# Issuing the next tile's q, k, v projection ahead of the feed-forward's down products in a two-layer transformer kernel

## The reference, cut to what matters

```python
def _layer(x, wqkv, qs, ksc, wo, lg, lb, w1, b1, w2, b2):
    h = shift_token(x)
    q, k, v = split(h @ wqkv, 3)            # 8 heads of 64
    q = l2norm(q) * qs ; k = l2norm(k) * ksc
    q, k = rotary_xpos(q, k)
    o = local_attention(q, k, v)            # windows of 64, each sees itself and the one before
    x = x + o @ wo
    h = layernorm(shift_token(x)) * lg + lb
    a, g = split(h @ w1 + b1, 2)            # hidden width 341
    return x + (a * gelu(g)) @ w2 + b2
```

## Time and profile before

| what | value |
|---|---|
| median of 3 runs | 470.61 us (469.17 to 472.55) |
| the profiled execution | 471.67 us |
| its span, first to last instruction | 469.9 us |
| granted TensorE clock, mean share | 0.916 |
| PE busy | 359.3 us (76%) |
| DVE busy | 329.7 us (70%) |
| POOL busy | 298.2 us (63%) |
| ACT busy | 285.0 us (61%) |

### The profile page before, as it was taken

How to read it: one execution, slowest core, us unless ns; L and a number is a source line. 1 busy time by engine, 2 the same in 40 slices (tenths; PEclk the granted TensorE clock), 3 DMA queues, 4 the chain that set the end, 5 groups by cost and what they waited for, 6 DMA issues and landing times.

```text
span 469.9 us, 11254 instructions
## 1 busy us (share of the span) xinstructions
PE 359.3 (76%) x3832; PEld 295.0 (63%) x3832; DVE 329.7 (70%) x744; ACT 285.0 (61%) x852; POOL 298.2 (63%) x248
## 2 busy tenths in 40 slices
PE   2573057898788998899899989998949896768362
PEld 1352036777676877687778767876838775656342
DVE  6879864678668768867877796768767866743423
ACT  3453075777676777777867867767827773664020
POOL 2200348999999499949975994899477958520212
PEclk9996575999999999999999999999979999797857
DMA  8500230511431052115113320431015201200100
GB/s 274 174 0 0 53 110 19 125 30 30 108 79 31 1 146 61 28 29 152 30 30 105 79 58 1 130 79 31 12 38 130 55 1 28 64 12 1 23 22 22
DMA packets 42399, 28.21 MB, mean 60 GB/s; under 512 B 21700, under 2 KB 36598, under 8 KB 42358
## 3 DMA queue, kind: packets, MB, share of 16 engines
q1 hardware_dynamic: 42357, 27.68, 22.7%
HBM read 13.51 MB, written 3.15 MB: 35 GB/s over the span
## 4 chain that ended last, share of the span: by engine, by line
PE 38%; DVE 22%; POOL 17%; issue 10%; ACT 7%; DMA 3%; SPq 2%; DVEq 1%; POOLq 0%; ACTq 0%
POOL rn L483 6%; PE bank L717 5%; DVE h L1083 4%; PE bank L682 4%; PE bank L554 4%; DVE rot_sin L1059 4%; PE bank L550 4%; PE upper L666 3%; PE bank L551 3%; DVE rot_cos L1059 3%; POOL rot L519 3%; ACT probs L833 2%; POOL rot L504 2%; PE bank L610 2%; POOL rot L505 2%
## 5 line engine op out<-in xcount | busy, mean ns | idle before, releaser
L833 ACT ACTIVATE probs<-upper,neg_max 128x128 f32<-128x128 f32 x256 | 90.4, 369 | 62.6 <-DVE neg_max L1105 62.6
L483 POOL TENSOR_TENSOR rn<-floored,minus_half 128x16 f32<-128x16 f32 x32 | 93.8, 2930 | 2.7
L504 POOL TENSOR_TENSOR rot<-rot_cos,rot_sin 128x512 f32<-128x512 f32 x32 | 40.9, 1278 | 64.9 <-DVE rot_sin L1059 47.1
L1105 DVE TENSOR_REDUCE neg_max<-upper 128x4 f32<-128x512 f32 x64 | 43.1, 683 | 34.4 <-PE upper L666 34.4
L519 POOL TENSOR_TENSOR rot<-rot,rn 128x1024 f32<-128x1024 f32 x32 | 60.9, 1903 | 1.9
L550 PE MATMUL bank<-wqkv_hi,act_t_hi 128*128 128x512 f32 x96 | 44.2, 460 | 21.4 <-DVE o_tok L1117 13.3
L833 ACT ACTIVATION_READ_ACCUMULATOR probs<-upper,neg_max 128x1 f32 x256 | 52.9, 207 | 0.0
L1059 DVE TENSOR_TENSOR rot_cos<-bank,tab 128x512 f32<-128x512 f32 x64 | 43.6, 682 | 2.7 <-PE bank L554 2.2
L1059 DVE TENSOR_TENSOR rot_sin<-bank,tab 128x512 f32<-128x512 f32 x64 | 43.5, 680 | 0.0
L1066 DVE TENSOR_REDUCE ss<-sq 128x16 f32<-128x1024 f32 x32 | 38.8, 1212 | 5.2 <-ACT sq L854 5.1
L550 PEld LDWEIGHTS bank<-wqkv_hi,act_t_hi 128*128 128x128 f32 x96 | 19.0, 198 | 36.0 <-issue 23.3
(11 more groups left out here) (129 smaller groups left out, 883.1 us busy)
## 6 DMA issues: line engine op xcount, KB each, us to landing
v_mid<-v_tok SPq DMA_DIRECT2D x64, 128.0 KB, 2.3
tab_raw<-tables SPq DMA_DIRECT2D x8, 512.0 KB, 3.3
h_tok<-group_in SPq DMA_DIRECT2D x14, 128.0 KB, 3.4
x_res<-group_in SPq DMA_DIRECT2D x28, 64.0 KB, 1.8
wqkv_raw<-wqkv SPq DMA_DIRECT2D x2, 768.0 KB, 6.7
x_in<-x SPq DMA_DIRECT2D x4, 256.0 KB, 3.4
head_scale<-head_scales SPq DMA_DIRECT2D x8, 128.0 KB, 3.9
group_in<-normed SPq DMA_DIRECT2D x4, 256.0 KB
```

The costliest lines, as they stand in the source:

```text
L483: pool.tensor_tensor(rn[:, 0:2 * HEADS], floored[:, 0:2 * HEADS], minus_half[:, :], ALU.pow).then_inc(rn_ready, 1)
L504: pool.tensor_tensor(rot[cur.par][:, :, 0:32], rot_cos[:, :, 0:32], rot_sin[:, :, 32:64], ALU.add).then_inc(rot_added, 1)
L833: last = act.activation(probs[:, h, :], s_bank[half][:, (h % 4) * P:(h % 4 + 1) * P], ACT.Exp, bias=neg_max[a.par][:, h:h + 1], accum_out= ...
```

## The change

In the passes that have a feed-forward (G of 1 and more) and a valid tile 4G+6, `project_qkv` of that tile is issued by PE inside `feed_forward`, behind the up products and ahead of the down products, and no longer at the head of stage j = 3. It waits there for the second gate (which frees banks 0 and 1) and the third gelu (bank 2). ACT squares q and k of the tile right behind the third gelu, ahead of the exponentials of stage 3, and no longer waits for `rotate`; DVE rotates the tile between the gates and `finish_group`, and waits for the squares instead, bank by bank. The copy of v, the sums of squares and everything on POOL and SP stay where they were.

```diff
             def feed_forward(F, layer, t_now, ahead):
...
                     last.then_inc(up_done, 1)
 
+                if ahead.valid:
+                    pe.wait_ge(gated_done, 3 * F + 2)
+                    pe.wait_ge(gelu_done, 3 * F + 3)
+                    project_qkv(ahead)
 
                 for c, (c0, cn) in enumerate(CHUNKS):
                     pe.wait_ge(gated_done, 3 * F + c + 1)
...
-                    if cur.valid:
+                    if cur.valid and not (j == 3 and not (number and G < 1)):
                         project_qkv(cur)
...
                         feed_forward(G - 1, (G - 1) // GROUPS if number else layer, cur.t + 1 if not number
-                                     else min(cur.t + 1, DEPTH * TILES + 4))
+                                     else min(cur.t + 1, DEPTH * TILES + 4), At(G, 3, 0, layer))
...
+            def squares(a, ready, n):
+                need(act, ss_ready, a.t)
+                for half, (b, s) in enumerate(zip((q_bank, k_bank), ready)):
+                    act.wait_ge(s, n)
+                    act.activation(sq[:, half * INNER:(half + 1) * INNER], b[:, :], ACT.Square).then_inc(squared, 1)
...
+                    early = j == 3 and not (number and G < 1)
...
-                        need(act, ss_ready, cur.t)
-                        for n, (b, read) in enumerate(((q_bank, q_rot), (k_bank, k_rot))):
-                            act.wait_ge(read, 2 * (cur.t + 1))
-                            act.activation(sq[:, n * INNER:(n + 1) * INNER], b[:, :], ACT.Square).then_inc(squared, 1)
+                        if not early:
+                            squares(cur, (q_rot, k_rot), 2 * (cur.t + 1))
...
                             act.activation(gelu_g[0:cn, c, :], up_bank[c][1][0:cn, :], ACT.Gelu,
                                            bias=b1_sb[l][0:cn, 3 + c:4 + c]).then_inc(gelu_done, 1)
+                        ahead = At(G, 3, 0, layer)
+                        if ahead.valid:
+                            squares(ahead, (q_done, k_done), ahead.t + 1)
...
-            def rotate(a):
+            def rotate(a, after_squares=False):
...
                     dve.wait_ge(ready, a.t + 1)
+                    if after_squares:
+                        dve.wait_ge(squared, 2 * a.t + 1 + n)
...
-                    if cur.valid:
+                    if cur.valid and not (j == 3 and not (number and G < 1)):
                         rotate(cur)
...
                             gate(G - 1, l, c, cn)
+                        ahead = At(G, 3, 0, layer)
+                        if ahead.valid:
+                            rotate(ahead, True)
                         finish_group(G - 1, l)
```

More of the change, by code:

```diff
@@ L690, in transpose_h2, with feed_forward @@
                 last.then_inc(h2t_done, 1)
-            def feed_forward(F, layer, t_now):
+            def feed_forward(F, layer, t_now, ahead):
                 taken = min(t_now, DEPTH * TILES) if isinstance(F, int) else t_now
```

## The result

The changed kernel takes 478.64 us (median of 4 runs, 478.27 to 478.93) against 471.58 us before (the three runs that were known, and a fourth): ratio 1.0155, 95% interval 1.0125 to 1.0184. It is slower by 7.1 us; its profiled execution has a span of 476.6 us against 469.9.

A forecast was written before the change was run, and what follows sets the result against it. PE's and POOL's paths arrive almost together in windows 1 to 4, POOL's alone binds 5 and 6; 3.7 plus 0.9 gives +4.6 us on the median 470.61: 475.2 us, range 469.0 to 479.2.

The forecast's parts named there:

- the credit for POOL's wait in windows 1 to 4: PE's transposes of q and k no longer wait for POOL: 0.49, 0.49, 0.43 and 0.22 us taken off.
- The group period: Sign in the profile after: a group of the first layer takes 44.4 us in place of 43.5.
- PE gap: Between up products and early projection PE waits for the third gelu and restarts slowly: 1.03 us lost per window.
- ACT: Squares run behind the gelu, the 1.28 us table load stays before the exponentials, which end at 252.26, not 249.91, in window 3.
- PE's delay: At the probabilities' transposes, whose second half waits for the exponentials, PE and all it feeds come 1.33 us late.
- DVE and POOL: DVE's copy beside POOL's sums takes up to 1.3 us; POOL's 1.3 head start is spent waiting, floored 0.47 later.
- The sum, windows 1 to 4: PE 1.33 late each, less its vanished wait for POOL: 0.84, 0.84, 0.90 and 1.11, together 3.7 us lost.
- ACT's slack (0.52 us): PE's idle time before the attention values, waiting for ACT's copies, 0.52 us, was to absorb POOL's lateness one stage later.
- The sum, windows 5 and 6: Second layer: only POOL's path counts, 0.47 us each, 0.9 together; PE's lateness hidden under 6.42 us idle.
- C: Rival: POOL is late too and binds the next stage's rotation, so no credit for its wait; 477.1 to 479.1 us, chance 0.20.
- B: Rival: exponentials not late, table load before the squares or hidden; +2.5 to +3.4, 473 to 474 us, chance 0.20.
- D: Rival: faster, POOL's path up to 1.3 us shorter per window if sums of squares are in time; 463 to 467, chance 0.07.

The follow-up runs named there:

- late_squares: Changed kernel with ACT's squares behind the exponentials again and DVE rotating without waiting for them, PE's order kept: 474.67 us, 1.0076 of the kernel before.
- preload: Changed kernel with one 128x1 exponential ahead of ACT's squares, so the table load runs earlier: 476.80 us, 1.0126 of the kernel before.
- all_three: Changed kernel with down products of chunks 0 and 1 before the projection, squares behind exponentials, early-tile copy behind sums of squares: 467.44 us, 0.9916 of before.
- busy_after: Changed kernel with 20 needless matmuls in PE's long idle time of windows 5 and 6: 476.24 us, 1.0113 of the kernel before.
- busy_before: Kernel before the change with 20 needless matmuls in PE's long idle time of windows 5 and 6: 471.31 us, 0.9987 of the kernel before.
- two_downs_first: Changed kernel with the down products of chunks 0 and 1 ahead of the projection, ACT's order as changed: 484.93 us, 1.0296 of the kernel before.
- squares_only: Changed kernel with PE's old order (all downs, then projection), ACT's and DVE's order as changed: 493.90 us, 1.0463 of the kernel before.
- copy_late: Changed kernel with DVE's copy of the two early tiles moved behind the sums of squares: 479.30 us, 1.0170 of the kernel before.

## Why the prediction was right or wrong, point by point

It put 475.2 us on a median of 470.61, and "within 1%" (0.53) ahead of "slower" (0.40). The measured time is 1.55% over before: inside the range, but slower, on the side that it held the less likely. The loss was 1.5 times the sum, and the step behind this is the credit for POOL's wait in windows 1 to 4, below. Of the signs that it put down all came: the gap, the load between squares and exponentials, the second half of the transposes waiting for ACT, POOL idle ahead of floored, the longer copy. The group period was 44.4 to 45.1, not 44.4, and floored started 10.05 us after the up products' end, where a start before 9.5 would have spoken against it.

- **PE gap**, 1.03 lost: right. The projection started 0.11 behind the gelu (0.06 put down), and the first half of the transposes 1.03 later than before. late_squares has the gap without ACT's part.
- **ACT**, the load staying in front of the exponentials: right, exponentials to 6.46 behind the gelu put down, 6.43 measured; preload hides the load and PE gets 0.4 us of it where nothing else binds.
- **PE's delay** of 1.33: 1.45 measured. The transposes' second half ends at 255.43, 7.29 behind the gelu, against 5.84. The refill behind the exponentials was late by 0.1.
- **DVE and POOL**: copy 1.27 (put at the upper bound), floored 9.34 (put at 9.25), POOL's head start spent waiting 1.61 us: right. POOL's sums started 1.13 sooner in window 3 and not 1.3.
- **The sum, windows 1 to 4, is the step that failed.** It subtracts the whole wait for POOL from PE's delay. "At its transposes of q and k it no longer waits for POOL" was right, and the credit was had there in all four windows: PE is 1.42 to 1.45 late ahead of these transposes, and 0.92, 0.85, 1.01 and 1.12 behind them. But in windows 1 and 4 it was handed back a step on, at the attention values. Window 1 before (third gelu at 158.51) and after (158.66):

```profile
173.16 0.58 ACT L858 COPY probs_t<-upper 128x512 f32<-128x512 f32 x1
...
174.23 0.27 PE L682 MATMUL bank<-v_mid,probs_t 128*64 128x64 f32 x1
```

```profile
174.73 0.58 ACT L867 COPY probs_t<-upper 128x512 f32<-128x512 f32 x1
...
175.65 0.27 PE L682 MATMUL bank<-v_mid,probs_t 128*64 128x64 f32 x1 [0.28 <-ACT probs_t L867]
...
176.73 0.66 PE L601 MATMUL bank<-const,h_tok 128*128 128x128 f32 x4
```

  Window 2 of the changed kernel, with the copy at 219.69, has no such wait:

```profile
219.69 0.58 ACT L867 COPY probs_t<-upper 128x512 f32<-128x512 f32 x1
...
220.33 0.27 PE L682 MATMUL bank<-v_mid,probs_t 128*64 128x64 f32 x1
```

  In windows 1 and 4 PE starts the values 0.33 us behind the end of ACT's copy, in windows 2 and 3 0.05 us behind it, and this pair stays the same in late_squares and all_three. Before the change PE came 0.49 behind it in window 1 and 0.36 in window 4, held back by POOL: ACT's path had only 0.16 and 0.03 us of slack, and these bound what the vanished wait could give. That ACT is 1.4 us late itself isn't needed for this: in all_three, where it isn't late, PE waits there by 0.28 and 0.27 too, and gains 0.16 and 0.06 where windows 2 and 3 gain 0.53 and 0.37. What fills the 0.33 us no run tests. In the code the stage behind windows 1, 4 and 5 stands in a loop over the passes, where PE's waits compare with computed values, and the one behind windows 2 and 3 is written out; busy_after has the 0.28 in window 5 as well.

  PE reads the next inputs 1.26, 0.92, 1.08 and 1.42 us late, and that is what the windows lose: 1.27, 0.92, 1.10 and 1.44 in place of 0.84, 0.84, 0.90 and 1.11, together 4.7 for 3.7. The 1.0 between them is 0.64 handed back in windows 1 and 4 and 0.14 in 2 and 3, and 0.42 of PE's delay above 1.33, less 0.21 by which the credit was larger than put down. I had looked for ACT's slack (0.52 us) only one stage further on.
- **The sum, windows 5 and 6**: 1.06 and 0.78 for 0.47 each. POOL's path is 0.55 late, close to the term. Of the other 0.5 in window 5, busy_after takes 0.2 to the low clock; the rest lies in the load of the inputs, which landed later, and isn't settled. Where PE waits for that load in window 5, its start moved by 0.34 us between the profiles of the kernel before and of busy_before (24.38 and 24.72 behind the gelu), which issue it at the same time. Term 0.9, measured 1.8.
- **Rivals.** C gave 477.1 to 479.1, with the credit not had and POOL's path at 0.6. The time falls there, but C's mechanism doesn't hold: in windows 1 and 4 the wait for ACT's copy took the credit back, not POOL, which PE didn't wait for in that stage, and windows 2 and 3 kept it. That the time is C's is luck. B's timely exponentials are what late_squares makes of the kernel, and it still loses 0.8%. D asked for sums of squares in time. all_three has floored 0.93 sooner with PE and ACT not made late for it, and gains in each window, but 1.8 us from gelu 1 to 6, far from the 1.3 us per window that D gave at most.
- **The chances.** A sum at the edge of 1% with every unpriced cost on the slow side (refills, ACT's slack, the range of the copy) should have given "slower" more than 0.40. The range was said to leave out C's upper edge; at 479.2 it has it inside (479.1).

## What to carry to other kernels

When work is moved ahead in one engine's order, price what it is moved past on every engine: here an early projection took the filling out of PE's wait for a gelu and put squares and a table load in front of exponentials that PE needs. A head start for one engine (POOL) is worth nothing until its second input comes early too, so follow both inputs to their last releaser. A credit for a wait that disappears has to be followed through all waits of the stage behind it, since it is worth no more than the slack of the path that arrives next: here ACT's copy, with 0.16 and 0.03 us in two windows of four. Windows that look alike have to be read one by one for this.

## What the runs showed of the hardware

- Pauses of PE of about 1 us were followed by a halved clock, though not each time: in two_downs_first waits of 1.03 and 0.74 us, 0.66 us apart, were followed by some 3 us at half speed in windows 1, 2 and 4, and not in 3, 5 and 6 with the same pauses; in squares_only, with 1.93 and 0.74, in all six. Four needless matmuls in the pause of 0.74 kept the clock at 1.00 in the profiled execution. In the changed kernel a gap of 0.77 to 0.82 and a wait of 0.20 per window left it at 1.00 in windows 1 to 4.
- The stretch from the third gelu of window 6 to the next differs by the clock from execution to execution: 50.1 us at a granted 0.88 in its last 28 us before the change, 48.0 us in late_squares at 1.00 in the last 24, and 46.1 us at 1.00 throughout in busy_before. This is larger than most effects here, so the experiments were compared up to that gelu only. In the profiles of before and after it is at 0.86 and 0.87, so their row for window 6 can be compared.
- A 128x256 copy on DVE took 0.28 to 0.30 us with POOL at rest (before, copy_late). Where it started inside one of POOL's two sums, it ended 0.15 or 0.16 us behind the end of that sum (0.20 where only 0.1 us of it was left), in each of the 48 cases of eight runs: 1.02 to 1.27 us in the changed kernel, 0.92 in two_downs_first, 0.50 to 0.59 in late_squares, 1.38 in windows 1 and 2 of preload, and 0.29 to 0.32 in its windows 3 to 6, where the sum had under 0.2 us to go. So its price was the time that the sum had left.
